# Attention phase: VectorE splits both token tiles of the next pair before it takes the score maxima of the second batch

## What is computed

```
xn = modulate(layernorm(x))                       # per batch: scale and shift from t_emb
q, k, v = xn @ wq + bq, xn @ wk + bk, xn @ wv + bv  # 16 heads of 32
attn = softmax(q @ k.T / sqrt(32))                # 128 x 128 for each head
x = x + (attn @ v) @ wo + bo
x = x + gelu(modulate(layernorm(x)) @ w1 + b1) @ w2 + b2   # width 2048
```

## Time and profile before

| | |
|---|---|
| time before, median of 3 runs | 2100.23 us (2096.84 to 2104.54) |
| profiled execution: time / span of its instructions | 2101.9 us / 2100.1 us |
| granted TensorE clock, mean | 0.994 of full speed |
| PE busy, share of the span | 2017.5 us, 96% |
| PEld busy | 1664.4 us, 79% |
| DVE busy | 1304.9 us, 62% |
| ACT busy | 671.0 us, 32% |
| POOL busy | 361.1 us, 17% |

### The profile page before, as it was taken

How to read it: one execution, slowest core, us unless ns; L and a number is a source line. 1 busy time by engine, 2 the same in 40 slices (tenths; PEclk the granted TensorE clock), 3 DMA queues, 4 the chain that set the end, 5 groups by cost and what they waited for, 6 DMA issues and landing times. The chain is left out here.

```text
span 2100.1 us, 32126 instructions
## 1 busy us (share of the span) xinstructions
PE 2017.5 (96%) x10706; PEld 1664.4 (79%) x10706; DVE 1304.9 (62%) x2302; ACT 671.0 (32%) x2006; POOL 361.1 (17%) x427
## 2 busy tenths in 40 slices
PE   5889999999999998999999999989999999999999
PEld 4568888887777777888888888867888788788887
DVE  5657777676676657888888888863524435254422
ACT  3222233322222223555555454632212112121211
POOL 4223333322222211111111111110101101010100
PEclk9999999999999999999999999999999999999999
DMA  7545444444444433222232323240211202011000
GB/s 259 174 142 171 161 153 150 134 165 165 152 141 143 140 106 99 75 85 80 80 85 80 85 80 85 76 153 23 81 41 41 66 15 81 27 56 58 23 21 21
DMA packets 160217, 208.41 MB, mean 99 GB/s; under 512 B 12844, under 2 KB 92296, under 8 KB 158088
## 3 DMA queue, kind: packets, MB, share of 16 engines
q1 hardware_dynamic: 150728, 177.37, 26.5%
q0 software_dynamic: 9360, 29.96, 4.9%
q10 hardware_dynamic: 48, 0.00, 0.0%
HBM read 132.83 MB, written 57.67 MB: 91 GB/s over the span
## 5 line engine op out<-in xcount | busy, mean ns | idle before, releaser
L606 PE MATMUL mlp_y<-weights,mlp_h 128*128 128x512 f32 x1536 | 384.2, 400 | 30.7 <-DVE mlp_h L832 30.6
L606 PE MATMUL ffn_y<-weights,ffn_h 128*128 128x512 f32 x1536 | 377.6, 395 | 4.6 <-DVE ffn_h L832 4.6
L583 PE MATMUL mlp_m<-xn,weights 128*128 128x512 f32 x1536 | 370.5, 392 | 5.6 <-DVE xn L820 5.6
L583 PE MATMUL ffn_m<-xn,weights 128*128 128x512 f32 x1536 | 371.2, 391 | 4.6 <-PEq L145 2.8
L606 PEld LDWEIGHTS mlp_y<-weights,mlp_h 128*128 128x128 f32 x1536 | 290.2, 190 | 107.9 <-DVE mlp_h L832 25.5
L606 PEld LDWEIGHTS ffn_y<-weights,ffn_h 128*128 128x128 f32 x1536 | 288.0, 188 | 74.7 <-DVE ffn_h L832 6.3
L583 PEld LDWEIGHTS mlp_m<-xn,weights 128*128 128x128 f32 x1536 | 289.5, 189 | 69.5 <-DVE xn L820 6.0
L583 PEld LDWEIGHTS ffn_m<-xn,weights 128*128 128x128 f32 x1536 | 289.2, 188 | 68.4 <-issue 6.3
L830 DVE CAST ffn_h<-ffn_g 128x512 fp32r<-128x512 f32 x128 | 54.7, 427 | 350.4 <-ACT ffn_g L719 349.6
L719 ACT ACTIVATE ffn_g<-ffn_m,vecs 128x512 f32<-128x512 f32 x128 | 88.0, 688 | 516.1 <-PE ffn_m L583 509.7
L1197 PE MATMUL att_banks<-xn,weights 128*128 128x256 f32 x1536 | 196.6, 286 | 12.0 <-PEq L145 6.1
(11 more groups left out here) (136 smaller groups left out, 2136.8 us busy)
## 6 DMA issues: line engine op xcount, KB each, us to landing
x_tiles<-x SPq DMA_DIRECT2D x132, 256.0 KB, 2.8
x<-x_tiles SPq DMA_DIRECT2D x96, 256.0 KB, 2.1
mlp_bias<-gate_bias_rows POOLq DMA_DIRECT2D x64, 256.0 KB, 3.9
mlp_gate<-gate_rows SPq DMA_DIRECT2D x16, 1024.0 KB, 5.2
att_kdiag<-xn SPq DMA_DIRECT2D x128, 128.0 KB, 2.5
turned_squares<-mlp_xhat SPq DMA_DIRECT2D x62, 256.0 KB, 3.2
mlp_xmod<-turned_squares SPq DMA_DIRECT2D x62, 256.0 KB, 2.8
x_tiles<-in_x_dram SPq DMA_DIRECT2D x32, 256.0 KB, 4.9
```

The lines of the kernel that those rows point to most:

```text
L583: last = nc.tensor.matmul(m1_ps[:, c % 2, :], st.tiles[0](a, k, c), xn[:, parity, b, k, :], start=s == 0, stop=s == len(steps) - 1)
L606: last = nc.tensor.matmul(y_ps[:, tile, :], h[:, c % 2, a, tile * P:(tile + 1) * P], st.tiles[1](b, c), start=c == 0 and s == 0, stop=c == ...
```

## The change

Two lines trade places in DVE's `pair_step`: the split of tile 1 of the next pair comes ahead of the maxima of the first half of row 2n+1, where it stood between the two halves. It holds in all 16 pairs. No instruction is added or removed, and the other engines' programs are the same.

```diff
@@ -1510,8 +1510,8 @@
                 if before:
                     finish(row - 1, 1)
                 split_xn(n + 1, 0)
+                split_xn(n + 1, 1)
                 row_max(row + 1, 0)
-                split_xn(n + 1, 1)
                 row_max(row + 1, 1)
                 dve.wait_ge(piece_hi, n + 1)
```

## The result

The changed kernel took 2093.97 us, median of 20 runs, the kernel before 2101.49 us, median of 20 runs. The ratio is 0.9964 (95% interval 0.9952 to 0.9975), a gain of 7.5 us (5 to 10 us). The forecast was a gain of 8.4 us and 2092 us. The gain is clear of noise and smaller than 0.5%.

A forecast was written before the change was run, and what follows sets the result against it. TensorE was taken to bound the attention phase, waiting 0.60 us a pair on DVE's L1419. Over 14 pairs that gave -8.4 us, all other terms nothing: median from 2100.2 to 2091.8 us, say 2092; range 2087.5 to 2100.

The forecast's parts named there:

- What bounds the kernel, and the price of the wait: TensorE sets the attention phase's time; its wait on DVE's L1419 costs 0.60 us a pair, 8.4 us in 14.
- The split of tile 1: DVE's cast moves up to t0+1.40 (t0: tile 0's cast start), TensorE goes on at t0+3.00 unwaiting; 0.60 us gained a pair.
- The first half of the maxima: On DVE it moves down, L1440 at t0+3.71; ACT's exponentials start about 0.1 us later, covered by some 2 us: cost nothing.
- The second half and its queue: DVE's second L1440 ends 0.05 to 0.25 us later; key product 0's split, needed by product 2, keeps 0.34 us cover: no cost.
- POOL against the first L1440: POOL's add, if first, holds DVE's L1440; bounds: none of 14 pairs (8.4 us stays) or 4 (5.6 us); none taken.
- rival B: POOL's add comes first in part of the pairs: four held leave 5.6 us, 2094.6 us; eight leave 2.7 us; chance 0.20.
- The price of a held pair: If POOL's add comes first, TensorE waits 0.71 us at key product 2; the pair is 0.1 us slower than before.
- The signs named ahead: In the profile: L1419's wait gone, no new L1431 wait, none to four long first-half L1440, pair period 35.47 to 34.87 us.
- Last pair: First L1440 runs free at t0+3.71, the second ends with POOL's add as before; everything behind unchanged: 0 us.
- A: POOL's add comes ahead of the first L1440 in all 14 pairs: 3.9 us lost, 2104 us; chance 0.09.
- C: The wait wasn't the bound: something TensorE waits for next, such as ACT's copies, was hidden by it; 2100 us; chance 0.06.
- D: More than 8.4 us gained, only if DVE's earlier split frees something beyond this wait; chance 0.03.

The follow-up runs named there:

- nudged kernel: Changed kernel plus one small unused DVE reduction in the loop, ahead of the first half of the maxima; ratio 1.0038 against the kernel before.
- ACT kernel: Changed kernel with the negation of the maxima (L1440) done by ACT, no longer by DVE; 2092.09 us, ratio 0.9946 against the kernel before.
- POOL always behind: Changed kernel with POOL's bias add for tile 1 waiting for the first L1440 of that row; ratio 0.9966 against the kernel before.
- POOL always first: Changed kernel with DVE's first-half L1440 waiting until POOL's add of tile 1 is done; ratio 1.0048 against the kernel before.
- ACT kernel with its tail edit: ACT kernel with the last pair's low part of the last weight piece behind row 30's weighed-values split; 2091.64 us, ratio 0.9947 against the kernel before.

## Why the prediction was right, point by point

**What bounds the kernel, and the price of the wait.** Right. The gap between starts gave 0.60 us a pair, and in a pair that isn't held the period shrank by 0.63 us (35.47 to 34.84 us). The other 0.03 us lie behind the product that waited: from key product 0 to key product 1 it is 2.61 us now (1032.64 - 1030.03) and was 2.64 us. The 5.1 us of the matmul row would have been too little: with no pair held the traces give 8.8 us.

**The split of tile 1.** Right to 0.01 us: cast at t0+1.40, TensorE at t0+3.00, no wait. The row's idle time by ACT is 0.24 us where 0.33 us was forecast; the forecast counted from t0+1.07, when DVE could have started, and the row counts from the end of the subtraction before it.

**The first half of the maxima.** L1440 at t0+3.72 to 3.73, forecast 3.71; the exponentials started at t0+4.02 and not 3.92, hidden as said, since no wait of TensorE leads back to them.

**The second half and its queue.** The split of key product 0 was ready at 1033.40 + 0.48 - 1027.03 = t0+6.85, forecast 6.72 to 6.77. L1440 ended at t0+5.25, inside the forecast; behind it the chain took 1.60 us and not 1.51 us, since L1517 started at L1440's end, where in the rows of before it had started 0.08 us ahead of it. The cover held in every unheld pair, and was 0.24 us instead of 0.34 us: key product 2 starts at t0+7.15 there.

**POOL against the first L1440.** This is the step that failed. The mechanism was right, and my choice between the two bounds was wrong. I took the upper end, none of four pairs lost, "since [...] a POOL row's start need not be its first access". In the traces of the changed kernel and of the one with the swap in the loop only, every pair of the 14 in which POOL's row starts before L1440's is held (7 in all: 3, 2, 2) and none of the other 35 is. The nearest case on one side is 0.01 us (held), on the other side the pair with both starts at 855.60 (not held). The order of the rows' starts decides. Held, L1440 took 1.25 to 1.30 us. The other way round the price is small: with DVE first by at most 0.02 us the add took 1.30 to 1.31 us instead of 1.28 to 1.29 us, and not the 0.17 us more that I had written. That a whole add is waited for by an instruction of 0.17 us agrees with the Trainium skill ("SBUF — State Buffer", section Who interferes with whom), which I had weighed and set aside; its reading is rival B, and B is what the traces show. That B's 5.6 us lies next to the first trace's 5.9 us is luck: four pairs at 0.71 us and three at 0.95 us come to the same loss (2.84 and 2.85 us).

**The price of a held pair.** Mis-sized: 0.71 us in the sum, 0.95 us measured (35.79 against 34.84 us, mean of three). In the pair shown, with 0.97 us, it can be followed. L1431 ended at t0+7.96 and not 7.82, 0.05 us of it because POOL started at 3.72 and not 3.67, the rest because L1517 started 0.17 us after L1440, where I had taken 0.08 us. Key product 2 started at t0+8.02; in an unheld pair, counting 12 matmuls on from product 1, it starts at t0+7.15, so my 7.17 was good and the delay is 0.87 us. The last 0.10 us come behind it: in the trace of single matmuls the first start behind a pause is 0.22 us ahead of the second, and 0.12 us in a row without pause. At the next group of matmuls the whole is there: 1072.87 - 1061.87 = t0+11.00 against 1037.06 - 1027.03 = t0+10.03. That the row of the sum and the row of the trace both say 0.71 us is chance; the row's idle time leaves out 0.16 us of overlap and those 0.10 us. So a held pair costs 0.32 us against before, not 0.1 us.

**The number.** The two errors, three held pairs where I counted none and 0.95 us for each, are 2.9 us in the first trace. The traces of the changed kernel give a gain of 5.9 and 6.9 us in the 14 pairs. The times gave 7.5 us with an interval of 5 to 10 us, which holds my 8.4 us and B's 5.6 us alike, so that the median came close to the forecast is in part luck and says nothing for my choice.

**The signs named ahead.** L1419's wait is gone, tile 1's cast is where it should be, and three long first halves lie within "none or up to four". But a wait on L1431 did come, and the period, taken over the same nine pairs as in the forecast, is (1237.98 - 922.51) / 9 = 35.05 us and not 34.87 us: it shrank by 0.42 us, less than the 0.6 us below which I called myself wrong. Two of the nine pairs are held; without them it shrank by 0.63 us. By that sign the forecast is right for the pairs in which DVE comes first and wrong for the three in which POOL does.

**Last pair.** Right: L1440's second half ended with POOL's add, at t0+5.88 (1347.40 + 0.83 - 1342.35; before t0+5.77, with POOL 0.12 us earlier). The stretch behind it was 1.1 us longer, and the twelve matmuls of the projection account for 1.4 us (4.43 against 3.02 us) at the lowered clock. Whether the swap makes that drop likelier isn't shown: the kernel before has one trace, at 1.00.

**Rivals.** A (slower, 2104 us) was two tenths of a microsecond away: the nudged kernel makes it true, at 8 us more. B (part of the gain, 0.20) is what happened, with two or three pairs in a trace and not four. C and D have nothing left for them.

## What to carry to other kernels

Price a wait by the distance of starts with and without it, best up to a start well behind it, and not by the idle time in its row (0.36 us for 0.63 us, 0.71 us for 0.97 us), and do so for the wait that may take its place too. When a DVE instruction with its operands in SBUF is moved, look up what POOL runs at its new place: a held instruction costs the rest of POOL's, however small it is, and a race decided by hundredths of a microsecond is best taken out, by letting POOL wait (8.8 us in the traces) or by giving the instruction to an engine that POOL doesn't meet (also 8.8 us in those pairs, and some 1.6 us more in pair 0 and behind the last pair).

## What the runs showed of the hardware beyond that

- DVE's maximum over 128x1024 in PSUM ran 1.21 to 1.23 us beside POOL's add and without it, while a subtraction of two SBUF operands (L1517) went from 0.69 us to 0.76 to 1.00 us beside it, in the ACT kernel. The negation of 128x8 in SBUF, held for over 1.2 us on DVE, took 0.21 us on ACT in all 14 pairs, in 8 of which POOL's add had begun first.
- The twelve matmuls of the projection of row 30, in all nine traces, by the wait right ahead of them. The clock is the mean granted over their own time, a mix of the two levels where it lies between 0.5 and 1:

| kernel | wait ahead, us | granted clock | twelve matmuls, us |
|---|---|---|---|
| before | 2.44 | 1.00 | 3.02 |
| changed, first trace | 2.56 | 0.66 | 4.43 |
| changed, second trace | 2.37 | 0.50 | 5.49 |
| swap in the loop only | 2.48 | 0.63 | 4.61 |
| POOL always behind | 2.43 | 0.63 | 4.61 |
| nudge | 2.38 | 0.63 | 4.62 |
| POOL always first | 4.08 | 0.58 | 4.96 |
| ACT kernel | 1.54 | 0.63 | 4.59 |
| ACT kernel with its tail edit | 1.53 | 1.00 | 3.01 |

Where the clock fell, the twelve matmuls took 1.4 to 2.5 us more. The length of the wait alone doesn't sort them, and two traces of one kernel differ by 1.1 us.
